# Loading packed weight codes and their scales as separate transfers in a fused attention and FFN block

## The chip, the cores and the metric

The kernel runs on one core of one Trainium2 chip. The metric is the device time of one execution in microseconds (us), taken as the median of the timed runs. The changed kernel is to be compared with the kernel before on the same chip.

## What is computed

The input `x` has 4 x 512 tokens of 512 channels, 2048 tokens in all. A first half adds a chunked, gated linear attention of `layernorm(x)` to `x`. A second half adds a gated FFN whose weights are stored as 4-bit codes, two in an int32 word, with one float scale for each block of 32:

```python
def dequant_nvfp4(W_packed, scales, block=32):
    low, high = W_packed & 15, W_packed >> 4 & 15
    idx = jnp.stack([low, high], axis=-1).reshape(N, -1)
    vals = NVFP4_LUT[idx].reshape(N, K // block, block) * scales[:, :, None]
    return vals.reshape(N, K)

Wg, Wu = dequant_nvfp4(gate_W_packed, ...), dequant_nvfp4(up_W_packed, ...)   # 4096 x 512 each
Wd = dequant_nvfp4(down_W_packed, ...)                                        # 512 x 4096
gate, up = xt @ Wg.T, xt @ Wu.T
gelu = jnp.tanh(0.7978845608 * (gate + 0.044715 * gate ** 3)) * gate * 0.5 + gate * 0.5
out = (gelu * up) @ Wd.T
```

## The kernel before

Every engine has a hand-written order of instructions, and semaphores tie the engines together. The attention part takes roughly the first quarter of the span. After that the FFN runs in eight groups of 512 hidden units (g = 0 to 7). Matrices are held as pairs of float16 parts (high and low), and three matmuls stand for one product. From tile 16 on the FFN is walked in pairs of hidden tiles (`m` = 8 to 63, eight pairs to a group). In each pair TensorE (PE) computes for `gate` and then for `up` seven block products P1 to P7, Strassen-like, with the down projection's products (`seven`, from m = 18 on, L695; `down`, L735, before and at the end) between them. ScalarE (ACT) copies partial results out of PSUM (`snapshot`, L1019), VectorE (DVE) adds to them (`combine`, L1376) and applies `inter` (L1269), ACT applies the gelu (L898), DVE adds down results into the rows of X1 (`into_rows`, L1304), and GpSimd (POOL) makes the low parts (L1601). `operand_sums` (L1314 to L1319) makes four differences of the finished pair on DVE, from pair 16 on in 46 pairs.

The weights come in 48 chunks of 128 x 512 codes, six to a group, numbered k. For a chunk the sync engine (SP) loads the codes into `raw` and the scales into `scl` (256 KB each; the scales are 8 rows, each repeated 16 times), from k = 10 on always into the same buffers. DVE's `dq_bits(k)` turns codes into float16 bits in a PSUM bank in four operations on 128 x 512 (L1330, L1332, L1335, L1338), one of which writes back into `raw`. `dq_finish(k)` multiplies them with the scales in two operations (L1359). ACT and POOL then split them into parts.

The order on DVE in a pair m, cut to what matters, is: `combine("gate", "C11")`, `dq_finish(k)` if a chunk is finished in this pair, `combine("gate", "C22")`, two `into_rows`, `dq_bits(k + 1)` if a chunk is finished in the next pair, `combine("gate", "C12")`. Chunks are finished in the pairs with m % 8 = 2, 3, 5, 6, 7 and 0, so that in the pairs with m % 8 = 2, 5, 6 and 7 a finish and the bits of the next chunk stand in one pair. After C12, ACT runs the gelu of the even tile and then the snapshot of P6 of `up`, for which PE's P7 of `up` waits.

SP's queue also moves rows of X1 to DRAM and back, 1 MB each (`kept`): in a pair with odd m it stores the rows of n = m // 2 - 1 after the last down product of n has been added (L1842), waits for the store to land, and fills the freed rows with those of n + 2 (L1846). The rows of n + 2 are needed from pair 2n + 6 on, that is m + 3.

Of the kernel before, what the change touches and what calls it, by code (L numbers as in the profile page):

```python
# [8 lines left out]
ALU = mybir.AluOpType  # L9
# [63 lines left out]
SEVEN = tuple(range(8, 31))  # L73
SEVEN_PAIRS = tuple(m for n in SEVEN for m in (2 * n, 2 * n + 1))
# [34 lines left out]
def row_done(n, tt):  # L109

    return 4 * n + tt + 1 - (4 * len(SEVEN) if n > SEVEN[-1] else 0)


def seventh(n, name):

    return 7 * (n - SEVEN[0]) + IN_TURN.index(name) + 1
# [19 lines left out]
def second(k):  # L136
    return not plain(k) and k % 2 == 1
# [18 lines left out]
def finished_in(k):  # L156

    return k - 2 if k < 12 else 8 * (k // 6) + (-6, -5, -3, -2, -1, 0)[k % 6]


FINISHED = {finished_in(k): k for k in range(10, 48)}
# [17 lines left out]
def block_kernel(nc, x, wqkv, bqk, bv, wab, bab, codes, scales, out, cla, kept):  # L179
    with ExitStack() as ctx:  # L180
# [3 lines left out]
        def sem(name):  # L184
            return ctx.enter_context(nc.semaphore(name))

        X1 = sb("X1", [128, NT, 512], F32)
# [8 lines left out]
        fw = sb("fw", [128, 2, 512], F32)  # L196
# [16 lines left out]
        def two(ap):  # L213
            return ap.rearrange("p (s n) -> p s n", s=2)
# [19 lines left out]
        tsum = E2[:, 0:1024].rearrange("p (t n) -> p t n", t=4)  # L234
# [8 lines left out]
        raw, scl = [load[:, j, :] for j in (0, 2)], [load[:, j, :].bitcast(F32) for j in (1, 3)]  # L243
# [75 lines left out]
        def row(n, tt):  # L319

            return 4 * (n % 4 if n < 4 else n % 2) + tt
# [13 lines left out]
        def floats(k):  # L335

            return wfs[pair_count(k) % 2 if k >= 12 else 0]

        def place(k):
            return k % 2 if k < 10 else 0  # L340

        def loaded(k):
            return 32 * (k // 2 + 1 if k < 10 else k - 4)

        def last_half(cut):
            return PS[0 if cut.start else bank_of["dn", NI // 4 - 1, 3]][:, 0:256]
# [7 lines left out]
        s_wv = [sem(f"s_wv{k}") for k in range(4)]  # L354
        s_k0 = sem("s_k0")
        s_const, s_out = sem("s_const"), sem("s_out")
        s_chunk = [sem(f"s_chunk{k}") for k in range(2)]
        s_setup = sem("s_setup")
        s_stat = {tag: sem(f"s_stat_{tag}") for tag in ("n1", "n2")}
        s_rstd = {tag: sem(f"s_rstd_{tag}") for tag in ("n1", "n2")}  # L360
# [16 lines left out]
        s_ihi, s_ilov, s_ilop, s_dn, s_ev = (sem(n) for n in ("s_ihi", "s_ilov", "s_ilop", "s_dn", "s_ev"))  # L377
        s_dq, s_whi, s_wlo, s_wl1 = (sem(n) for n in ("s_dq", "s_whi", "s_wlo", "s_wl1"))
# [3 lines left out]
        s_dsum, s_ohi, s_olo, s_seven, s_out7 = (sem(n) for n in ("s_dsum", "s_ohi", "s_olo", "s_seven", "s_out7"))  # L382
        s_half, s_done = sem("s_half"), sem("s_done")
        s_kept = [sem(f"s_kept{b}") for b in (2, 3)]
        s_store = [sem(f"s_store{i}") for i in range(2)]
# [447 lines left out]
        def _(eng):  # L833
# [58 lines left out]
            def gelu(i, pg, at=0):  # L892
                if i // 2 - 1 in SEVEN_PAIRS:
                    ac.wait_ge(s_olo, operand(i // 2 - 1, "o"))
                    ac.wait_ge(s_dsum, 4 * (i // 2 - 1 - SEVEN_PAIRS[0]) + 4)
                elif i >= 2:
                    ac.wait_ge(*ilo(i - 2))
                eng.activation(fw[:, i % 2, at:at + pg.shape[1]], pg, ACT.Gelu_apprx_tanh, scale=GS).then_inc(s_gelu, 1)  # L898
# [25 lines left out]

            def sums_high(m):
                for part in ("T01", "T23"):
                    ac.wait_ge(s_dsum, 4 * (m - SEVEN_PAIRS[0]) + 4)
                    eng.copy(part_of(m, 0, part), part_from(part)).then_inc(s_ohi, 1)  # L928

            def act_tile(i):  # L930
# [189 lines left out]
        def _(eng):  # L1120
# [184 lines left out]
                                         1.0 / (WS * IS), block_, ALU.mult, ALU.add).then_inc(s_out7, 1)  # L1305

            def operand_sums(m):
                e, o, at = fw[:, 0, :], fw[:, 1, :], 4 * (m - SEVEN_PAIRS[0])
                if m > SEVEN_PAIRS[0]:
                    dv.wait_ge(s_olo, operand(m - 1, "T23"))  # L1310
                else:
                    dv.wait_ge(s_kept[0], 16)
                dv.wait_ge(s_inter, whole(2 * m))
                eng.tensor_tensor(tsum[:, 0, :], e[:, 256:512], e[:, 0:256], ALU.subtract).then_inc(s_dsum, 1)  # L1314
                eng.tensor_tensor(tsum[:, 2, :], o[:, 256:512], e[:, 256:512], ALU.subtract).then_inc(s_dsum, 1)
                dv.wait_ge(s_dsum, at + 1)
                eng.tensor_tensor(tsum[:, 1, :], o[:, 256:512], tsum[:, 0, :], ALU.subtract).then_inc(s_dsum, 1)  # L1317
                dv.wait_ge(s_dsum, at + 3)
                eng.tensor_tensor(tsum[:, 3, :], o[:, 0:256], tsum[:, 1, :], ALU.subtract).then_inc(s_dsum, 1)  # L1319

            def dq_bits(k):

                s, codes_ = place(k), codes_in(k)
                dv.wait_ge(s_chunk[s], loaded(k))
                if k:
                    dv.wait_ge(s_dq, 6 * k)
                if k == 6:
                    for sm7, value in freed7:
                        dv.wait_ge(sm7, value)
                eng.tensor_scalar(codes_, raw[s], 4097, None, ALU.mult).then_inc(s_dq, 1)  # L1330
                dv.wait_ge(s_dq, 6 * k + 1)
                eng.tensor_scalar(raw[s], codes_, 12, -0x7FFF8000, ALU.logical_shift_left,  # L1332
                                  ALU.bitwise_and).then_inc(s_dq, 1)
                dv.wait_ge(s_dq, 6 * k + 2)
                eng.tensor_scalar(codes_, codes_, 9, 0x0E000E00, ALU.logical_shift_left,  # L1335
                                  ALU.bitwise_and).then_inc(s_dq, 1)
                dv.wait_ge(s_dq, 6 * k + 3)
                eng.tensor_tensor(codes_, codes_, raw[s], ALU.bitwise_or).then_inc(s_dq, 1)  # L1338

            def dq_finish(k):  # L1340
                s, dst = place(k), wf2 if second(k) else floats(k)
                dv.wait_ge(s_dq, 6 * k + 4)
                if second(k):
                    dv.wait_ge(s_wlo, WLO[k - 1][1])
                    if k == 7:
                        dv.wait_ge(s_turn["n2"], NT)
                    dv.wait_ge(s_wsum, pair_count(k) - 1)
                elif k in (12, 14):
                    dv.wait_ge(s_kept[1], 16)
                    dv.wait_ge(s_wlo, WLO[11][1])  # L1350
                    dv.wait_ge(s_wsum, 2)
                elif k > 14:
                    dv.wait_ge(s_wsum, pair_count(k) - 2)
                elif k and second(k - 1):
                    dv.wait_ge(s_wsum, pair_count(k - 1))
                for nib in range(2):
                    if 0 < k < 12 and not second(k) and not second(k - 1):
                        dv.wait_ge(s_wlo, WLO[k - 1][nib])
                    eng.scalar_tensor_tensor(dst[:, nib, :], codes_in(k).bitcast(F16)[:, nib::2], CODE, scl[s],  # L1359
                                             ALU.mult, ALU.mult).then_inc(s_dq, 1)  # L1360
# [405 lines left out]
        def _(eng):  # L1766
# [8 lines left out]
            def load_w(j):  # L1775
                eng.dma_start(wsrc[j], wv[:, :, 512 * j:512 * j + 512].rearrange("k p n -> p k n")).then_inc(s_w[j], 16)

            def load_chunk(k):
                s = place(k)
                if k >= 2:  # L1780
                    sp.wait_ge(s_dq, 6 * (k - 2 if k <= 10 else k - 1) + 6)
                eng.dma_start(raw[s], codes[k // 6, k % 6]).then_inc(s_chunk[s], 16)
                src = scales[k // 6, k % 6]
                rep = bass.AP(src.tensor, src.offset, [[512, 8], [0, 16], [1, 512]])
                eng.dma_start(scl[s], rep).then_inc(s_chunk[s], 16)

            def load_rows(T):
                if T >= 4:
# [35 lines left out]
                load_chunk(k)  # L1824
            sp.wait_ge(s_ev, 12)
            eng.dma_start(kept[2], X1[:, 8:12, :]).then_inc(s_kept[0], 16)
            for m in range(8, NI // 2):
                for k in range(10, 47):
                    if finished_in(k) == m:
                        load_chunk(k + 1)  # L1830
                n = m // 2 - 1
                if m == 9:
                    sp.wait_ge(s_ev, 16)
                    eng.dma_start(kept[3], X1[:, 12:16, :]).then_inc(s_kept[1], 16)
                elif m % 2 and n < 30:
                    if n in SEVEN:
                        sp.wait_ge(s_out7, seventh(n, "P4"))
                    else:
                        sp.wait_ge(s_ev, row_done(n, 3))
                    half_of = X1[:, row(n, 0):row(n, 0) + 4, :]  # L1840
                    home = ov[4 * (n % 4):4 * (n % 4) + 4].rearrange("t p d -> p t d") if n >= 28 else kept[n % 4]
                    eng.dma_start(home, half_of).then_inc(s_store[n % 2], 16)  # L1842
                    sp.wait_ge(s_store[n % 2], 16 * ((n - 4) // 2 + 1))
                    if n < 6:
                        sp.wait_ge(s_kept[n % 2], 16)
                    eng.dma_start(half_of, kept[(n + 2) % 4]).then_inc(s_fill[n % 2], 16)  # L1846
            for T in range(8, NT - 1):
                n = NI // 4 - 4 + T // 4
                if n in SEVEN:
# [48 lines left out]
```

## Time and profile before

| | |
|---|---|
| median of 2 timed runs | 1288.96 us (1288.34 to 1289.59) |
| the profiled execution, its own time | 1286.35 us |
| its span, first to last instruction | 1284.6 us |
| mean granted TensorE clock | 0.955 |
| PE busy | 1160.0 us (90%) |
| DVE busy | 847.9 us (66%) |
| ACT busy | 490.2 us (38%) |
| POOL busy | 647.3 us (50%) |
| DMA: queue of SP | 95.23 MB, 20.6% of 16 engines |

Busy times are those of one profiled execution and are averages over its stages. The span and the time of that execution differ by 1.75 us, which lies around the first and last instruction. A granted clock of 1 is 2.4 GHz, and 0.5 is 1.2 GHz.

### The profile page before, as it was taken

To read this page: it belongs to the slowest core of one execution; us is meant where nothing else is said; L and a number is where in the kernel's file an instruction comes from. 1 tells how busy PE (TensorE), PEld (TensorE's weight loads), DVE (VectorE), ACT (ScalarE), POOL (GpSimd) and SP (SyncE) were. 2 spreads that over 40 slices of the span, in tenths; PEclk is the share of its full clock that TensorE was granted. 3 is DMA by queue.
4 is the path that set the end of the run, shared out by engine and by line. 5 is a ranking of instruction groups with operands and counts; after the bars stand their busy time and mean duration, and the time that the engine had idled before them with its cause. 6 is when DMAs were issued, how large, how long until landed. Compare 5 with 4: busy or idle time off the path is not lost.

```text
span 1284.6 us, 22355 instructions
## 1 busy us (share of the span) xinstructions
PE 1160.0 (90%) x8842; PEld 884.5 (69%) x8842; DVE 847.9 (66%) x1537; ACT 490.2 (38%) x1148; POOL 647.3 (50%) x665
## 2 busy tenths in 40 slices
PE   9999999999989797987988798978897898879999
PEld 5566555654656565875877677867686786768887
DVE  8788574577665456665767676766676666766664
ACT  4423442532434243433433343424343343335342
POOL 3476342457656355544644563635455473547330
PEclk9999999999999899997999998999999898989999
DMA  7021010001022222220221222222222121221222
GB/s 271 10 67 58 12 47 18 9 17 66 18 82 81 85 99 82 83 99 28 105 92 66 90 83 83 99 83 100 82 83 99 62 111 59 83 66 66 96 94 76
DMA packets 30233, 96.66 MB, mean 75 GB/s; under 512 B 3440, under 2 KB 3760, under 8 KB 23472
## 3 DMA queue, kind: packets, MB, share of 16 engines
q1 hardware_dynamic: 30128, 95.23, 20.6%
q8 instruction: 70, 1.15, 0.3%
q14 instruction: 35, 0.29, 0.1%
HBM read 63.73 MB, written 31.49 MB: 74 GB/s over the span
## 4 chain that ended last, share of the span: by engine, by line
PE 59%; DVE 20%; DMA 10%; issue 6%; ACT 4%; SPq 1%; POOL 0%; DVEq 0%; POOLq 0%
PE ps L626 23%; PE ps L695 9%; DMA load<-scales 9%; PE ps L456 8%; PE ps L587 6%; PE ps L735 6%; DVE X L1317 2%; DVE fw L1269 2%; DVE load L1376 2%; DVE load L1332 2%; DVE ps L1335 2%; DVE ps L1330 2%; ACT fw L898 2%; DVE X L1304 1%; DVE bigB L1376 1%
## 5 line engine op out<-in xcount | busy, mean ns | idle before, releaser
L626 PE MATMUL ps<-REG,bigA 128*128 128x256 f16 x672 | 103.4, 296 | 115.3 <-ACT bigB L1019 115.2
L626 PE MATMUL ps<-REG,WR 128*128 128x256 f16 x1344 | 193.6, 283 | 0.0
L626 PE MATMUL ps<-XT,WR 128*128 128x256 f16 x1344 | 184.0, 273 | 0.0
L1019 ACT COPY load<-ps 128x256 f32<-128x256 f32 x168 | 62.5, 372 | 282.1 <-PE ps L626 282.0
L626 PEld LDWEIGHTS ps<-REG,bigA 128*128 128x128 f16 x672 | 66.3, 104 | 138.5 <-ACT bigB L1019 127.0
L1376 DVE TENSOR_TENSOR bigB<-bigB,ps 128x256 f32<-128x256 f32 x168 | 69.9, 416 | 133.4 <-ACT bigB L1019 102.3
L1601 POOL TENSOR_TENSOR ihl_s<-fw,ihl_s 128x512 f16<-128x512 f32 (+1 forms) x46 | 49.0, 1077 | 208.1 <-ACT ihl_s L922 208.1
L626 PEld LDWEIGHTS ps<-REG,WR 128*128 128x128 f16 x1344 | 135.7, 102 | 26.1 <-issue 1.3
L626 PEld LDWEIGHTS ps<-XT,WR 128*128 128x128 f16 x1344 | 132.1, 98 | 16.1
L898 ACT ACTIVATE fw<-load 128x256 f32<-128x256 f32 x112 | 58.7, 524 | 181.7 <-DVE load L1376 181.4
L1304 DVE SCALAR_TENSOR_TENSOR X<-ps,X 128x512 f32<-128x512 f32 x161 | 108.0, 682 | 18.1 <-PE ps L695 15.7
L1019 ACT COPY bigB<-ps 128x256 f32<-128x256 f32 x168 | 62.1, 370 | 89.0 <-PE ps L626 89.0
L695 PE MATMUL ps<-WR,ihl_s 128*128 128x256 f16 x684 | 91.8, 276 | 1.5 <-DVE X L1290 1.5
L1269 DVE SCALAR_TENSOR_TENSOR fw<-fw,ps 128x256 f32<-128x256 f32 (+1 forms) x72 | 34.4, 478 | 79.9 <-PE ps L626 47.9
L456 PE MATMUL ps<-XT,WR 128*128 128x512 f16 x384 | 86.8, 379 | 0.0
L1330 DVE TENSOR_SCALAR ps<-load 128x512 int32<-128x512 int32 x42 | 29.0, 691 | 86.0 <-DMA load<-scales 85.9
L1376 DVE TENSOR_TENSOR load<-load,ps 128x256 f32<-128x256 f32 x168 | 68.4, 410 | 25.8 <-ACT load L1019 19.0
L587 PE MATMUL ps<-XT,WR 128*128 128x512 f16 x384 | 85.0, 379 | 0.0
L1601 POOL TENSOR_TENSOR vv<-fw,vv 128x256 f16<-128x256 f32 (+1 forms) x46 | 42.4, 934 | 75.7 <-ACT vv L922 75.7
L1601 POOL TENSOR_TENSOR ihl_s<-X,ihl_s 128x512 f16<-128x512 f32 x46 | 52.9, 1161 | 48.5 <-ACT ihl_s L928 48.5
L695 PEld LDWEIGHTS ps<-WR,ihl_s 128*128 128x128 f16 x684 | 67.6, 99 | 10.3 <-DVE X L1290 1.8
L1269 DVE SCALAR_TENSOR_TENSOR fw<-fw,bigB 128x256 f32<-128x256 f32 x112 | 70.1, 626 | 3.9
(232 smaller groups left out, 2540.7 us busy)
## 6 DMA issues: line engine op xcount, KB each, us to landing
kept<-X SPq DMA_DIRECT2D x26, 1024.0 KB, 4.0
X<-kept SPq DMA_DIRECT2D x26, 1024.0 KB, 4.8
load<-codes SPq DMA_DIRECT2D x48, 256.0 KB
load<-scales SPq DMA_DIRECT2D x48, 256.0 KB
bigA<-cla SPq DMA_DIRECT2D x14, 256.0 KB, 3.1
X<-x SPq DMA_DIRECT2D x3, 1024.0 KB, 13.1
WR<-wqkv SPq DMA_DIRECT2D x2, 1024.0 KB, 9.7
y<-X SPq DMA_DIRECT2D x2, 1024.0 KB, 4.7
```

The costliest lines, as they stand in the source:

```text
L456: mm = eng.matmul(PS[bank][:, :], lhs, rhs, start=(n == 0), stop=(n == 11))
L587: mm = eng.matmul(bank[:, :], buf[:, wp, o + kt, 128 * j:128 * j + 128], XT[:, xp, kt, 512 * b:512 * b + 512], start=(n == 0), stop=(n == 11))
L626: mm = eng.matmul(half_bank(kind, name), w(wp, kt), x(xp, kt), start=(first and n == 0), stop=(n == 5), skip_group_check=True)
L695: mm = eng.matmul(PS[bank][:, 256 * tt:256 * tt + 256], x, weight(wp, u), start=(name in ("P1", "P2", "P5") and tt == u == ip == wp == 0), ...
L735: mm = eng.matmul(PS[bank][:, :], ih[:, ip, 128 * tt:128 * tt + 128], buf[:, wp, at(j), :], start=(j == 0 and p == 0), stop=(j == end and ...
L898: eng.activation(fw[:, i % 2, at:at + pg.shape[1]], pg, ACT.Gelu_apprx_tanh, scale=GS).then_inc(s_gelu, 1)
L1019: eng.copy(start, half_bank(kind, name)).then_inc(s_snap, 1)
L1269: eng.scalar_tensor_tensor(w, w, GS * IS, pu, ALU.mult, ALU.mult).then_inc(s_inter, 1)
L1304: eng.scalar_tensor_tensor(block_, PS[bank][:, :].rearrange("p (t u n) -> p t u n", t=2, u=2), 1.0 / (WS * IS), block_, ALU.mult, ALU.add) ...
L1330: eng.tensor_scalar(codes_, raw[s], 4097, None, ALU.mult).then_inc(s_dq, 1)
L1376: eng.tensor_tensor(c, c, half_bank(kind, end), ALU.add).then_inc(s_comb, 1)
L1601: eng.tensor_tensor(part_of(m, 1, part), part_from(part), part_of(m, 0, part), ALU.subtract).then_inc(s_olo, 1)
```

## The change

The codes and the scales of a chunk get a semaphore each, and are issued in separate steps. `dq_bits` waits for the codes alone and `dq_finish` for the scales alone. The codes of chunk k + 1 are issued as soon as `dq_bits(k)` is through (from k = 10 on), and no longer after `dq_finish(k)`. The scales of chunk k + 1 are still issued after `dq_finish(k)`. On SP the fill of rows moves from the odd pair, right behind its store, into the next pair, behind that pair's scales. Besides that, two of the four subtractions of `operand_sums` on 128 x 256 become one on 128 x 2 x 256, and its semaphore counts three steps and not four.

```diff
         def loaded(k):
-            return 32 * (k // 2 + 1 if k < 10 else k - 4)
+            return 16 * (k // 2 + 1 if k < 10 else k - 4)
...
             def operand_sums(m):
...
-                eng.tensor_tensor(tsum[:, 0, :], e[:, 256:512], e[:, 0:256], ALU.subtract).then_inc(s_dsum, 1)
-                eng.tensor_tensor(tsum[:, 2, :], o[:, 256:512], e[:, 256:512], ALU.subtract).then_inc(s_dsum, 1)
+                eng.tensor_tensor(tsum[:, 0::2, :], fw[:, :, 256:512], two(e), ALU.subtract).then_inc(s_dsum, 1)
                 dv.wait_ge(s_dsum, at + 1)
                 eng.tensor_tensor(tsum[:, 1, :], o[:, 256:512], tsum[:, 0, :], ALU.subtract).then_inc(s_dsum, 1)
-                dv.wait_ge(s_dsum, at + 3)
+                dv.wait_ge(s_dsum, at + 2)
                 eng.tensor_tensor(tsum[:, 3, :], o[:, 0:256], tsum[:, 1, :], ALU.subtract).then_inc(s_dsum, 1)
...
             def dq_bits(k):
-                dv.wait_ge(s_chunk[s], loaded(k))
+                dv.wait_ge(s_codes[s], loaded(k))
...
             def dq_finish(k):
                 s, dst = place(k), wf2 if second(k) else floats(k)
+                dv.wait_ge(s_scales[s], loaded(k))
...
-            def load_chunk(k):
+            def load_codes(k):
+                s = place(k)
+                if k >= 2:
+                    sp.wait_ge(s_dq, 6 * (k - 2) + 6 if k <= 10 else 6 * (k - 1) + 4)
+                eng.dma_start(raw[s], codes[k // 6, k % 6]).then_inc(s_codes[s], 16)
+
+            def load_scales(k):
                 s = place(k)
                 if k >= 2:
                     sp.wait_ge(s_dq, 6 * (k - 2 if k <= 10 else k - 1) + 6)
-                eng.dma_start(raw[s], codes[k // 6, k % 6]).then_inc(s_chunk[s], 16)
                 src = scales[k // 6, k % 6]
                 rep = bass.AP(src.tensor, src.offset, [[512, 8], [0, 16], [1, 512]])
-                eng.dma_start(scl[s], rep).then_inc(s_chunk[s], 16)
+                eng.dma_start(scl[s], rep).then_inc(s_scales[s], 16)
...
             for m in range(8, NI // 2):
-                for k in range(10, 47):
-                    if finished_in(k) == m:
-                        load_chunk(k + 1)
                 n = m // 2 - 1
+                if m < 10:
+                    load_codes(m + 3)
+                    load_scales(m + 3)
+                if m == 10:
+                    load_codes(13)
+                if m >= 10 and m in FINISHED and FINISHED[m] < 47:
+                    load_scales(FINISHED[m] + 1)
+                if m % 2 == 0 and 4 <= n - 1 < 30:
+                    fill_rows(n - 1)
+                if m >= 10 and m + 1 in FINISHED and FINISHED[m + 1] < 47:
+                    load_codes(FINISHED[m + 1] + 1)
...
                 elif m % 2 and n < 30:
-                    if n in SEVEN:
-                        sp.wait_ge(s_out7, seventh(n, "P4"))
-                    else:
-                        sp.wait_ge(s_ev, row_done(n, 3))
...
-                    sp.wait_ge(s_store[n % 2], 16 * ((n - 4) // 2 + 1))
...
-                    eng.dma_start(half_of, kept[(n + 2) % 4]).then_inc(s_fill[n % 2], 16)
+                    store_rows(n)
```

`store_rows` and `fill_rows` hold the same waits and transfers as the lines taken out.

SP's queue before, for pairs 21 to 23. `load<-codes` (L1782) and `load<-scales` (L1785) are a chunk's two transfers, first those of chunk 21. `kept<-X` is the store and `X<-kept` the fill; `s_dq` is the count that `dq_bits` and `dq_finish` raise.

```order
L1782 DMA load<-codes 128x512 [waits s_dq]
L1785 DMA load<-scales 128x1x512
L1842 DMA kept<-X 128x2048 [waits s_out7]
L1846 DMA X<-kept 128x2048 [waits s_store1]
L1782 DMA load<-codes 128x512 [waits s_dq]
L1785 DMA load<-scales 128x1x512
L1782 DMA load<-codes 128x512 [waits s_dq]
L1785 DMA load<-scales 128x1x512
L1842 DMA kept<-X 128x2048 [waits s_out7]
L1846 DMA X<-kept 128x2048 [waits s_store0]
```

The same pairs in the changed kernel; codes are now L1783, scales L1791, the store L1847, the fill L1853.

```order
L1791 DMA load<-scales 128x1x512 [waits s_dq]
L1783 DMA load<-codes 128x512 [waits s_dq]
L1847 DMA kept<-X 128x2048 [waits s_out7]
L1791 DMA load<-scales 128x1x512 [waits s_dq]
L1853 DMA X<-kept 128x2048 [waits s_store1]
L1783 DMA load<-codes 128x512 [waits s_dq]
L1791 DMA load<-scales 128x1x512 [waits s_dq]
L1783 DMA load<-codes 128x512 [waits s_dq]
L1847 DMA kept<-X 128x2048 [waits s_out7]
```

The scales of chunk 21 now stand ahead of the codes of chunk 22, which wait for `dq_bits(21)`; the codes of chunk 21 have been issued in pair 20. The fill has moved past the scales of pair 22.

DVE in pair 22 before, from `operand_sums` of pair 21 to `dq_bits(22)`: L1317 and L1319 are its last subtractions, L1376 the combines, L1359 `dq_finish(21)`, L1304 `into_rows`, and L1330 the first operation of `dq_bits(22)`.

```order
L1314 TENSOR_TENSOR X<-fw 128x256 [waits s_inter,s_olo]
L1315 TENSOR_TENSOR X<-fw 128x256
L1317 TENSOR_TENSOR X<-fw,X 128x256 [waits s_dsum]
L1319 TENSOR_TENSOR X<-fw,X 128x256 [waits s_dsum]
L1376 TENSOR_TENSOR load<-load,ps 128x256 [waits s_prod,s_snap]
L1359 SCALAR_TENSOR_TENSOR bigC<-ps,load 128x512 [waits s_wsum,s_wlo,s_dq]
L1359 SCALAR_TENSOR_TENSOR bigC<-ps,load 128x512
L1376 TENSOR_TENSOR load<-load,ps 128x256 [waits s_snap]
L1304 SCALAR_TENSOR_TENSOR X<-ps,X 128x4x128 [waits s_fill0,s_seven]
L1304 SCALAR_TENSOR_TENSOR X<-ps,X 128x4x128 [waits s_out7,s_seven]
L1330 TENSOR_SCALAR ps<-load 128x512 [waits s_dq,s_chunk0]
```

The same stretch in the changed kernel, where the lines from L1315 on are those of the new text.

```order
L1315 TENSOR_TENSOR X<-fw 128x2x256 [waits s_inter,s_olo]
L1317 TENSOR_TENSOR X<-fw,X 128x256 [waits s_dsum]
L1319 TENSOR_TENSOR X<-fw,X 128x256 [waits s_dsum]
L1377 TENSOR_TENSOR load<-load,ps 128x256 [waits s_prod,s_snap]
L1360 SCALAR_TENSOR_TENSOR bigC<-ps,load 128x512 [waits s_wlo,s_wsum,s_dq,s_scales0]
L1360 SCALAR_TENSOR_TENSOR bigC<-ps,load 128x512
L1377 TENSOR_TENSOR load<-load,ps 128x256 [waits s_snap]
L1305 SCALAR_TENSOR_TENSOR X<-ps,X 128x4x128 [waits s_fill0,s_seven]
L1305 SCALAR_TENSOR_TENSOR X<-ps,X 128x4x128 [waits s_out7,s_seven]
L1330 TENSOR_SCALAR ps<-load 128x512 [waits s_dq,s_codes0]
```

One instruction less stands there, `s_chunk0` at L1330 has become `s_codes0`, the first L1360 waits for `s_scales0` as well, and nothing else on DVE has changed places.

## Rows read from the trace of the kernel before

**Rows 1.** The cores' view: span and mean granted TensorE clock.

```profile
core 0: 1284.6 us, clock 0.955
```

**Rows 2.** The waits of the whole span: us in total, times, longest us.

```profile
PE ps L626 <- ACT bigB L1019: 115.2, 35, 7.2
...
DVE ps L1330 <- DMA load<-scales: 85.9, 24, 7.3
```

**Rows 3.** Timeline of pair 22: start us, us, engine; idle before and its releaser in brackets.

```profile
568.25 0.42 DVE L1314 TENSOR_TENSOR X<-fw 128x256 f32<-128x256 f32 x1
...
568.88 1.96 POOL L1601 TENSOR_TENSOR vv<-fw,vv 128x512 f16<-128x512 f32 x2 [10.63 <-ACT vv L922]
...
568.93 1.38 DVE L1317 TENSOR_TENSOR X<-fw,X 128x256 f32<-128x256 f32 x1
...
570.64 0.32 SPq L1846 DMA_DIRECT2D X<-kept  x1
...
571.37 1.27 DVE L1359 SCALAR_TENSOR_TENSOR bigC<-ps,load 128x512 f32<-128x512 f16 x2
...
572.67 0.33 SPq L1782 DMA_DIRECT2D load<-codes  x1
...
573.05 0.63 SPq L1785 DMA_DIRECT2D load<-scales  x1
...
577.74 0.69 DVE L1330 TENSOR_SCALAR ps<-load 128x512 int32<-128x512 int32 x1 [3.36 <-DMA load<-scales]
...
579.92 0.70 DVE L1338 TENSOR_TENSOR ps<-ps,load 128x512 int32<-128x512 int32 x1
...
580.98 0.63 ACT L898 ACTIVATE fw<-load 128x512 f32<-128x512 f32 x1 [5.68 <-DVE load L1376]
...
581.92 1.46 PE L626 MATMUL ps<-REG,bigA 128*128 128x256 f16 x6 [3.76 <-ACT bigB L1019]
```

**Rows 4.** Busy time by stretch: pairs 22, 25, 37, and pairs 58 and 59.

```profile
568.90:590.10 21.20, 17.44 (x136) 14.24 (x135) 12.91 (x24) 6.40 (x16) 10.24 (x10) 0.84 0.27 97
...
625.10:639.50 14.40, 13.63 (x126) 11.89 (x125) 11.39 (x22) 7.42 (x18) 9.97 (x10) 1.00 0.09 35
...
826.40:843.60 17.20, 13.32 (x123) 11.60 (x122) 12.26 (x24) 5.96 (x15) 6.64 (x7) 1.00 0.15 58
1191.50:1218.80 27.30, 27.30 (x252) 24.34 (x251) 17.77 (x34) 10.80 (x27) 8.43 (x9) 1.00 0.20 73
```

**Rows 5.** Busy time by stretch: the eight pairs 25 to 32, summed.

```profile
sum 137.00, PE 117.30 PEld 100.68 DVE 93.82 ACT 53.30 POOL 72.76; mean PE 29.33 PEld 25.17 DVE 23.45 ACT 13.32 POOL 18.19
```

**Rows 6.** PE busy in the 22 stretches at clock 0.5: first three, sum.

```profile
372.40:375.80 3.40, 3.13 (x11) 0.50 0.02 5
406.50:410.00 3.50, 3.50 (x14) 0.51 0.00 0
440.70:447.50 6.80, 3.99 (x13) 0.50 0.00 0
...
sum 116.20, PE 90.47; mean PE 4.11
```

**Rows 7.** Timeline of PE, 385 to 486 us: two of the stalls at P7.

```profile
405.54 0.83 PE L626 MATMUL ps<-REG,bigA 128*128 128x256 f16 x6 [2.47 <-ACT bigB L1019]
423.13 0.83 PE L626 MATMUL ps<-REG,bigA 128*128 128x256 f16 x6 [1.38 <-ACT bigB L1019]
```

**Rows 8.** Timeline of 340 to 386 us: bits of chunk 12, and PE behind them.

```profile
367.45 0.69 DVE L1330 TENSOR_SCALAR ps<-load 128x512 int32<-128x512 int32 x1 [2.44 <-DMA load<-scales]
...
372.67 1.46 PE L626 MATMUL ps<-REG,bigA 128*128 128x256 f16 x6 [4.79 <-ACT bigB L1019]
```

**Rows 9.** L1317 by source line: duration ns min/median/max.

```profile
L1317 DVE TENSOR_TENSOR X<-fw,X x46: 417/1382/1386, 481.4 to 1246.3; 128x256 f32<-128x256 f32 x46
```

**Rows 10.** Timeline of DVE, 980 to 984 us: the one short L1317, and L1319.

```profile
981.27 0.42 DVE L1317 TENSOR_TENSOR X<-fw,X 128x256 f32<-128x256 f32 x1
981.72 1.26 DVE L1319 TENSOR_TENSOR X<-fw,X 128x256 f32<-128x256 f32 x1
```

More of the change, by code:

```diff
@@ L356, in block_kernel @@
         s_const, s_out = sem("s_const"), sem("s_out")
-        s_chunk = [sem(f"s_chunk{k}") for k in range(2)]
+        s_codes = [sem(f"s_codes{k}") for k in range(2)]
+        s_scales = [sem(f"s_scales{k}") for k in range(2)]
         s_setup = sem("s_setup")
@@ L894, in gelu @@
                     ac.wait_ge(s_olo, operand(i // 2 - 1, "o"))
-                    ac.wait_ge(s_dsum, 4 * (i // 2 - 1 - SEVEN_PAIRS[0]) + 4)
+                    ac.wait_ge(s_dsum, 3 * (i // 2 - 1 - SEVEN_PAIRS[0]) + 3)
                 elif i >= 2:
@@ L926, in sums_high @@
                 for part in ("T01", "T23"):
-                    ac.wait_ge(s_dsum, 4 * (m - SEVEN_PAIRS[0]) + 4)
+                    ac.wait_ge(s_dsum, 3 * (m - SEVEN_PAIRS[0]) + 3)
                     eng.copy(part_of(m, 0, part), part_from(part)).then_inc(s_ohi, 1)
@@ L1307, in operand_sums @@
             def operand_sums(m):
-                e, o, at = fw[:, 0, :], fw[:, 1, :], 4 * (m - SEVEN_PAIRS[0])
+                e, o, at = fw[:, 0, :], fw[:, 1, :], 3 * (m - SEVEN_PAIRS[0])
                 if m > SEVEN_PAIRS[0]:
@@ L1781, in load_chunk @@
                     sp.wait_ge(s_dq, 6 * (k - 2 if k <= 10 else k - 1) + 6)
-                eng.dma_start(raw[s], codes[k // 6, k % 6]).then_inc(s_chunk[s], 16)
                 src = scales[k // 6, k % 6]
                 rep = bass.AP(src.tensor, src.offset, [[512, 8], [0, 16], [1, 512]])
-                eng.dma_start(scl[s], rep).then_inc(s_chunk[s], 16)
+                eng.dma_start(scl[s], rep).then_inc(s_scales[s], 16)
+            def load_chunk(k):
+                load_codes(k)
+                load_scales(k)
             def load_rows(T):
@@ L1826, in _, with home_of, store_rows, fill_rows @@
             eng.dma_start(kept[2], X1[:, 8:12, :]).then_inc(s_kept[0], 16)
+            def home_of(n):
+                if n >= 28:
+                    return ov[4 * (n % 4):4 * (n % 4) + 4].rearrange("t p d -> p t d")
+                return kept[n % 4]
+            def store_rows(n):
+                if n in SEVEN:
+                    sp.wait_ge(s_out7, seventh(n, "P4"))
+                else:
+                    sp.wait_ge(s_ev, row_done(n, 3))
+                eng.dma_start(home_of(n), X1[:, row(n, 0):row(n, 0) + 4, :]).then_inc(s_store[n % 2], 16)
+            def fill_rows(n):
+                sp.wait_ge(s_store[n % 2], 16 * ((n - 4) // 2 + 1))
+                if n < 6:
+                    sp.wait_ge(s_kept[n % 2], 16)
+                eng.dma_start(X1[:, row(n, 0):row(n, 0) + 4, :], kept[(n + 2) % 4]).then_inc(s_fill[n % 2], 16)
             for m in range(8, NI // 2):
-                for k in range(10, 47):
-                    if finished_in(k) == m:
-                        load_chunk(k + 1)
                 n = m // 2 - 1
+                if m < 10:
[9 more added lines that the diff above has]
+                    load_codes(FINISHED[m + 1] + 1)
                 if m == 9:
@@ L1835, in _ @@
                 elif m % 2 and n < 30:
-                    if n in SEVEN:
-                        sp.wait_ge(s_out7, seventh(n, "P4"))
-                    else:
-                        sp.wait_ge(s_ev, row_done(n, 3))
-                    half_of = X1[:, row(n, 0):row(n, 0) + 4, :]
-                    home = ov[4 * (n % 4):4 * (n % 4) + 4].rearrange("t p d -> p t d") if n >= 28 else kept[n % 4]
-                    eng.dma_start(home, half_of).then_inc(s_store[n % 2], 16)
-                    sp.wait_ge(s_store[n % 2], 16 * ((n - 4) // 2 + 1))
-                    if n < 6:
-                        sp.wait_ge(s_kept[n % 2], 16)
-                    eng.dma_start(half_of, kept[(n + 2) % 4]).then_inc(s_fill[n % 2], 16)
+                    store_rows(n)
             for T in range(8, NT - 1):
```

## The prediction

> **What bounds the kernel now.** I read the cores' view first: the span is 1284.6 us and the mean granted clock of TensorE is 0.955 [rows 1]. With only two levels, 1 and 0.5, that mean says that TensorE ran at 1.2 GHz for 2 x 0.045 x 1284.6 = 116 us. Both numbers of the story are there: PE is the engine with the most work, and it loses time to stalls and to a lowered clock.
>
> Then the waits [rows 2]. PE waits for one thing above all: 115.2 us in 35 stalls behind ACT's copy of P6 of `up`. DVE waits 85.9 us in 24 pieces at L1330, the first operation of `dq_bits`, for the DMA. The reader should ask whether these are the same time, and the timeline of pair 22 answers that [rows 3]. `dq_finish` starts at 571.37 and takes 1.27 us; only then, at 572.67 and 573.05, does SP issue the next chunk's codes and scales, which are through at 577.74, some 4.7 us after the second issue. DVE has stood still for 3.36 us by then. Four operations of bits follow, the last at 579.92, then C12, the gelu on ACT at 580.98, the snapshot, and PE resumes at 581.92 after a stall of 3.76 us. So the DMA wait stands inside PE's stall, and 3.76 - 3.36 = 0.40 us of the stall would be left without it.
>
> The stretches tell what a pair costs when nothing is late: pairs 58 and 59, in which nothing is dequantized, take 27.3 us together at full clock with PE always busy, 13.65 us each [rows 4]. Pair 22 takes 21.2 us at a mean clock of 0.84. Pair 25, which has bits and no finish just ahead of them, takes 14.4 us with 0.77 us of PE idle. This tells me that the bits alone cost little and the late transfer much.
>
> **The change, part by part.**
>
> *The codes' wait.* `dq_bits(k + 1)` stands in the same pair as `dq_finish(k)` in half of the pairs. Before, the load between them could not start until the finish was over. Now the codes are issued when `dq_bits(k)` is through, a pair earlier, some 14 us ahead at a pair's length of 14.4 us [rows 4], against less than 5 us that two transfers took [rows 3]. What SP moves past: the codes of the next chunk stand behind the scales (which wait for the finish, at the start of the pair) and, in even pairs, behind the fill, whose store was issued in the odd pair before; all of these come earlier in a pair than the bits, so the queue holds nothing up. The first of the waits is at 367.45, for chunk 12, 2.44 us inside a stall of 4.79 [rows 8]; there the codes are issued after the bits of chunk 11 and no longer after its finish, about 2 us sooner and without the scales behind them, so that I count it too. All 24 waits go: 85.9 us. In four of them PE's stall was shorter than DVE's wait, by up to 0.3 us (in the longest 7.2 against 7.3 [rows 2]), which takes off 0.9. **Term one: 85.0 us.** What is late next is DVE's own chain, 115.2 - 85.0 = 30 us of stall over 35 places, under 1 us each.
>
> *The clock.* The 22 stretches at 0.5 hold 116.2 us, in 90.47 of which PE was busy [rows 6]. Work done at half the clock takes twice as long, so half of the busy part is lost: 45.2 us. All but two of these stretches lie in or right behind a stall that held a DMA wait of those above. The two are the one at 406.50, behind a stall of 2.47 us that no DMA wait made [rows 6, 7], and the first one, at 372.40, where 4.79 - 2.44 = 2.35 us of stall stay [rows 8]; I leave both as they are, 3.13 and 3.50 us busy. That gives (90.47 - 6.63) / 2 = 41.9. I take the full value, since the stalls that stay are of the size of the one of 1.38 us at 423.13, after which no fall comes until 440.70, and since even 17.20 - 13.32 = 3.88 us of idle in pair 37 left the clock at 1.00 [rows 4, 6, 7]. **Term two: 41.9 us**, with 0 as its low end and 45.2 as its high end. As a check, pair 22 at clock 0.84 was slow for 0.16 x 2 x 21.2 = 6.8 us and so lost up to 3.4: 21.2 - 3.4 - 3.4 = 14.4 us or a little more, which is what pair 25 takes.
>
> *The fill.* It is issued in the next pair behind the scales, some 2 us later than the 570.64 of pair 22 [rows 3]. Its rows are needed three pairs, over 40 us, after the store's. Nothing: what hides it is these pairs, and were that cover gone the first `into_rows` would wait the 2 us.
>
> *The scales.* Issued as before, needed at the next finish, a pair or two on. Nothing is queued behind that wait that doesn't need it. 0.
>
> *The joined subtraction.* Before, L1314 starts at 568.25 and takes 0.42, and its twin runs until just past 568.93, where L1317 starts. An operation on 128 x 512 takes 0.70 (L1338) [rows 3], so the joined one ends at 568.95, and L1317 starts as before. L1317 then takes 1.38 us (median of 46 [rows 9]) because POOL's L1601 began at 568.88; that stays. I take 0, since the two starts differ by 0.02 us. The ends: in one pair L1317 came ahead of POOL, and it and L1319 took 0.42 + 1.26 = 1.68 us and not 2.15 [rows 10]. If the change brought that order, it would gain 0.47 us in each of the 30 pairs in which DVE's chain holds PE (20 with finish and bits, 10 with bits alone), 14 us. If the joined operation ran into POOL as L1317 does, it would cost 1.38 - 0.42 = 0.96 us there, 29 us.
>
> **The sum.** 85.0 + 41.9 = 126.9 us. Span: 1284.6 - 126.9 = 1157.7; that execution's own time 1286.35 - 126.9 = 1159.4. The median of the runs lies 2.6 us above that execution, so the forecast is **1162 us**. Is there room on the other engines? Eight pairs took 137.0 us with 93.8 us of DVE and 72.8 of POOL [rows 5]. The 126.9 us come out of some 800, so eight pairs shrink to about 115 us: DVE is then 82% busy and POOL 63%, and PE's floor is 8 x 13.65 = 109. Close, but nothing crosses.
>
> **The rivals.**
>
> *The clock doesn't recover.* Short stalls may go on lowering it: the one of 2.47 us did [rows 7]. The 30 us of stall that stay are spread over 35 places. Against it are the 1.38 us without a fall and pair 25 at 1.00 with its 0.77. If term two is nothing: 1162 + 42 = 1204; if half: 1183. The Trainium skill, "TensorE: Matmul & The Clock Gate", in its section on a second failure mode, tells of a kernel whose clock swung because PE idled briefly but often between groups of matmuls; by that rule this rival's 1204 would be the result. The rows at hand speak against it. Chance 0.10.
>
> *The joined subtraction collides with POOL*: 1162 + 29 = 1191. For it: 45 of 46 L1317 did collide. Against it: the joined one starts 0.6 us ahead of POOL [rows 3]. Chance 0.06.
>
> *The change doesn't do what it says*: codes are held back on SP, so that half of the waits and their falls stay, for instance in even pairs where the fill stands ahead of them. 1289 - 63 = 1226. The store had landed by 570.64, well ahead of the bits, which speaks against it. Chance 0.05.
>
> *Another engine takes over* (DVE's 82% leaves chains that don't fit) and the gain falls under 26 us: 1263 to 1289, chance 0.02.
>
> *Slower*: the finish now waits for scales alone, at the head of the pair, ahead of everything on DVE. With 37 finishes after the loads are split, a loss that eats the 127 us and more needs 3.4 us at each, that is scales that land over 14.4 + 3.4 = 18 us after their issue; the slowest thing seen is both transfers within 5 us [rows 3]. Beyond 18 us the kernel is slower than 1289. Chance 0.02.
>
> **How the numbers follow.** The forecast case, 0.75, is 1162 with ends from its own bounds: 14 us for the subtraction and 3.3 for the two kept falls below give 1145, and a third of term two above gives 1176. The range of 8 in 10 reaches on to the collision and to a half-recovered clock: 1145 to 1192; what lies above is half of the clock's case and the last three, 0.14. A measurement of this kernel can tell about 2% from no change, that is 1263 us: faster 0.95, the same 0.03, slower 0.02.
>
> **What would show it.** Right: no DMA wait at L1330, codes issued some 10 us ahead of their bits; PE's wait behind L1019 near 30 us; pairs with finish and bits at 14.3 to 15.2 us; mean clock about 0.99; L1317 still at 1.38 and L1315 at 0.70. Wrong in term two: waits gone and the clock at 0.96 or below. Wrong in the subtraction: L1315 at over 1 us. Wrong in the queue: SP issuing a chunk's codes less than 5 us ahead of its bits. The step that I trust least is that stalls of 1 to 2 us leave the clock alone.

## The result

The changed kernel takes 1159.74 us (median, 1159.74 to 1159.75) against 1288.96 us before. The ratio is 0.8998 with a 95% interval of 0.8959 to 0.9036: faster by 10%, 2.3 us from the forecast of 1162.

The cores' view of the changed kernel, beside [rows 1]:

```profile
core 0: 1157.6 us, clock 0.999
```

The waits of the whole span, beside [rows 2] (us in total, times, longest us). L1019 has become L1020 and L626 L627.

```profile
PE ps L627 <- ACT bigB L1020: 30.0, 31, 2.5
```

No line of DVE waiting for a DMA at L1330 is left. PE's stall behind ACT's copy has gone from 115.2 to 30.0 us, and the clock from 0.955 to 0.999. These are the two terms of the result, the stall and the clock; what follows shows how they hang together. The lines below are those of the profiled execution, 1159.75 us.

The timeline of pair 22, beside [rows 3]:

```profile
533.43 0.33 SPq L1783 DMA_DIRECT2D load<-codes  x1
...
539.06 0.69 DVE L1315 TENSOR_TENSOR X<-fw 128x512 f32<-128x512 f32 x1
...
539.78 1.34 DVE L1317 TENSOR_TENSOR X<-fw,X 128x256 f32<-128x256 f32 x1
...
542.19 1.27 DVE L1360 SCALAR_TENSOR_TENSOR bigC<-ps,load 128x512 f32<-128x512 f16 x2
...
543.49 0.63 SPq L1791 DMA_DIRECT2D load<-scales  x1
...
544.16 0.45 SPq L1853 DMA_DIRECT2D X<-kept  x1
...
545.11 0.68 DVE L1330 TENSOR_SCALAR ps<-load 128x512 int32<-128x512 int32 x1
...
547.28 0.70 DVE L1338 TENSOR_TENSOR ps<-ps,load 128x512 int32<-128x512 int32 x1
...
548.01 0.33 SPq L1783 DMA_DIRECT2D load<-codes  x1
...
548.33 0.63 ACT L899 ACTIVATE fw<-load 128x512 f32<-128x512 f32 x1 [2.52 <-DVE load L1377]
...
549.28 0.83 PE L627 MATMUL ps<-REG,bigA 128*128 128x256 f16 x6 [0.64 <-ACT bigB L1020]
```

The codes that `dq_bits` reads at 545.11 were issued at 533.43, 11.7 us ahead, in the pair before. The bits follow the rows' additions with no idle time, and PE's stall is 0.64 us and no longer 3.76. Six matmuls take 0.83 us and not 1.46: the clock is up.

Busy time by stretch: the only fall left, pairs 22 and 25, the eight pairs 25 to 32, pair 37, pairs 58 and 59, beside [rows 4 to 6]:

```profile
371.00:374.40 3.40, 3.40 (x13) 1.57 (x11) 0.84 (x2) 0.43 (x2) 0.73 (x1) 0.50 0.03 5
539.80:555.00 15.20, 14.56 (x134) 12.75 (x133) 13.30 (x22) 6.30 (x16) 10.22 (x10) 1.00 0.42 141
584.30:598.70 14.40, 13.63 (x126) 11.91 (x124) 11.34 (x20) 7.40 (x18) 9.97 (x10) 1.00 0.15 55
584.30:700.90 116.60, 111.30 (x1011) 97.45 (x1009) 93.90 (x161) 53.33 (x126) 72.81 (x66) 1.00 0.28 100
758.50:772.90 14.40, 13.30 (x123) 11.56 (x121) 12.09 (x22) 5.94 (x15) 6.61 (x7) 1.00 0.21 72
1064.50:1091.80 27.30, 27.30 (x253) 24.34 (x251) 17.70 (x31) 10.79 (x27) 8.42 (x9) 1.00 0.19 72
```

Pair 22 went from 21.2 to 15.2 us, pair 37, where no fall was to be recovered, from 17.2 to 14.4, and pair 25 and pairs 58 and 59, which had no DMA wait, took as long as before. Eight pairs take 116.6 us and not 137.0, with the same work on DVE (93.9) and POOL (72.8).

PE's row of the changed kernel's page splits the gain without any estimate, since PE has the same 8842 matmuls in both kernels:

```profile
PE 1117.3 (97%) x8842; PEld 862.1 (74%) x8842; DVE 848.7 (73%) x1491; ACT 489.4 (42%) x1148; POOL 646.9 (56%) x665
```

Its busy time fell from 1160.0 to 1117.3 us, which is 42.7 us for the same work, and the time in which it stood idle from 1284.6 - 1160.0 = 124.6 to 1157.6 - 1117.3 = 40.3 us, which is 84.3.

### The profile page after: what moved, and what is told of

It is laid out like the page before. It is cut to its first block, busy times and chain, and to the rows that moved or that the text cites. A ratio compares the mean times of both kernels' runs of the same rounds, so it can differ in the third digit from the quotient of the medians.

```text
span 1157.6 us, 22346 instructions
## 1 busy us (share of the span) xinstructions
PE 1117.3 (97%) x8842; PEld 862.1 (74%) x8842; DVE 848.7 (73%) x1491; ACT 489.4 (42%) x1148; POOL 646.9 (56%) x665
## 4 chain that ended last, share of the span: by engine, by line
PE 63%; DVE 24%; issue 7%; ACT 4%; DMA 1%; POOL 0%; DVEq 0%; SPq 0%; POOLq 0%
PE ps L627 24%; PE ps L696 9%; PE ps L457 9%; PE ps L588 7%; PE ps L736 7%; DVE X L1305 3%; DVE X L1317 3%; DVE fw L1270 3%; DVE load L1377 3%; DVE load L1332 2%; DVE ps L1335 2%; DVE ps L1330 2%; ACT fw L899 2%; DVE X L1315 2%; DVE bigB L1377 1%
## 5 line engine op out<-in xcount | busy, mean ns | idle before, releaser
L627 PE MATMUL ps<-REG,WR 128*128 128x256 f16 x1344 | 183.9, 273 | 0.0
L627 PE MATMUL ps<-XT,WR 128*128 128x256 f16 x1344 | 183.3, 273 | 0.0
L1020 ACT COPY load<-ps 128x256 f32<-128x256 f32 x168 | 62.5, 372 | 248.0 <-PE ps L627 247.9
L627 PEld LDWEIGHTS ps<-REG,WR 128*128 128x128 f16 x1344 | 130.4, 98 | 21.5 <-issue 0.6
L627 PEld LDWEIGHTS ps<-XT,WR 128*128 128x128 f16 x1344 | 131.5, 98 | 15.5
L627 PE MATMUL ps<-REG,bigA 128*128 128x256 f16 x672 | 92.0, 273 | 30.2 <-ACT bigB L1020 30.0
L627 PEld LDWEIGHTS ps<-REG,bigA 128*128 128x128 f16 x672 | 62.4, 98 | 49.1 <-ACT bigB L1020 40.6
L1020 ACT COPY bigB<-ps 128x256 f32<-128x256 f32 x168 | 62.1, 369 | 77.9 <-PE ps L627 77.9
L1270 DVE SCALAR_TENSOR_TENSOR fw<-fw,bigB 128x256 f32<-128x256 f32 x112 | 74.4, 665 | 3.9
L1270 DVE SCALAR_TENSOR_TENSOR fw<-fw,ps 128x256 f32<-128x256 f32 (+1 forms) x72 | 34.3, 477 | 50.4 <-PE ps L588 30.0
L588 PEld LDWEIGHTS ps<-XT,WR 128*128 128x128 f16 x384 | 37.6, 98 | 44.4
```

What stands on the lines that cost most here:

```text
L588: mm = eng.matmul(bank[:, :], buf[:, wp, o + kt, 128 * j:128 * j + 128], XT[:, xp, kt, 512 * b:512 * b + 512], start=(n == 0), stop=(n == 11))
L627: mm = eng.matmul(half_bank(kind, name), w(wp, kt), x(xp, kt), start=(first and n == 0), stop=(n == 5), skip_group_check=True)
L1020: eng.copy(start, half_bank(kind, name)).then_inc(s_snap, 1)
L1270: eng.scalar_tensor_tensor(w, w, GS * IS, pu, ALU.mult, ALU.mult).then_inc(s_inter, 1)
```

## The experiments

**The joined subtraction alone.** The kernel before with this and its counts:

```diff
-eng.tensor_tensor(tsum[:, 0, :], e[:, 256:512], e[:, 0:256], ALU.subtract).then_inc(s_dsum, 1)
-eng.tensor_tensor(tsum[:, 2, :], o[:, 256:512], e[:, 256:512], ALU.subtract).then_inc(s_dsum, 1)
+eng.tensor_tensor(tsum[:, 0::2, :], fw[:, :, 256:512], two(e), ALU.subtract).then_inc(s_dsum, 1)
...
```

> The kernel before with the joined subtraction alone. Theory (it costs nothing): 1289 us within 3, L1315 (the joined one) at 0.69 us and L1317 at about 1.34, ending when it did before. Rival (it runs into POOL's operation): 0.96 us more in 30 pairs, 1318 us. Rival (DVE gets ahead of POOL): 0.47 us less in 30 pairs, 1275 us.

1285.71 us (1280.57 to 1290.59), ratio to the kernel before 0.9982 (0.9961 to 1.0003): no change that can be told. By source line (duration ns min/median/max), the joined operation and then the next one:

```profile
L1314 DVE TENSOR_TENSOR X<-fw x46: 691/692/693, 478.5 to 1249.9; 128x512 f32<-128x512 f32 x46
```

```profile
L1316 DVE TENSOR_TENSOR X<-fw,X x46: 426/1336/1344, 479.2 to 1250.6; 128x256 f32<-128x256 f32 x46
```

The second still takes 1.34 us in the median; the shortest of 46 takes 0.43, against 0.42 before [rows 9]. In the changed kernel the two run from 539.06 to 539.78 + 1.34 = 541.12, 2.06 us; before, from 568.25 to 568.93 + 1.38 = 570.31, 2.06 us [rows 3]. Both rivals fall: one wanted 29 us more, the other 14 less.

**A semaphore each, nothing moved.** The kernel before, where `dq_bits` waits for the codes and `dq_finish` for the scales, but both are still issued after the last finish:

```diff
-eng.dma_start(raw[s], codes[k // 6, k % 6]).then_inc(s_chunk[s], 16)
+eng.dma_start(raw[s], codes[k // 6, k % 6]).then_inc(s_codes[s], 16)
...
-eng.dma_start(scl[s], rep).then_inc(s_chunk[s], 16)
+eng.dma_start(scl[s], rep).then_inc(s_scales[s], 16)
```

> The kernel before with a semaphore each for codes and scales and nothing moved: both are still issued after the finish of the last chunk. Theory (what costs is that the codes are issued late, and the scales behind them add a part): codes are through some 1.5 us before both are, so DVE waits 85.9 - 24 x 1.5 = 50 us, and about half of the clock's 42 us comes back: 1289 - 36 - 20 = 1233 us. Rival (codes and scales share the DMA engines and end together): 1285 us or more. Rival (the shared semaphore was all of it): 1162 us.

1233.90 us, ratio 0.9578 (0.9536 to 0.9620), as expected. Its waits:

```profile
PE ps L627 <- ACT bigB L1020: 81.3, 33, 5.8
...
DVE ps L1331 <- DMA load<-codes: 50.4, 22, 5.9
```

The wait falls from 85.9 to 50.4 us by the semaphore alone: the scales behind the codes had made up 35.5 us of it.

**Codes early, but the bits wait for both.** The changed kernel with

```diff
             def dq_bits(k):
                 dv.wait_ge(s_codes[s], loaded(k))
+                dv.wait_ge(s_scales[s], loaded(k))
```

> The changed kernel, but the bits wait for the scales of their chunk too. Theory (the scales are issued at the end of the finish and need some 3.5 us, the bits want them 1.6 us after their issue): DVE waits about 1.9 us at L1330 in some 20 pairs, 40 us, with few falls of the clock since the stalls stay near 3 us: 1160 + 40 to 1160 + 60, 1200 to 1220 us. Rival (the codes were all that was late, the order on SP does it): 1160 us.

1234.40 us, ratio 0.9575 (0.9544 to 0.9606), 14 us above the upper end of what was expected. Its waits:

```profile
PE ps L627 <- ACT bigB L1020: 78.9, 35, 4.1
...
DVE ps L1331 <- DMA load<-scales: 26.2, 14, 2.6
...
DVE ps L1331 <- issue: 21.9, 10, 2.4
```

The second line of DVE is the same wait, for which the profile names no releaser. Its timeline, pair 23:

```profile
574.17 0.63 SPq L1792 DMA_DIRECT2D load<-scales  x1
...
577.91 0.69 DVE L1331 TENSOR_SCALAR ps<-load 128x512 int32<-128x512 int32 x1 [2.24 <-issue]
```

So DVE waits 48 us and not 40, PE's stall is 48.9 us above the changed kernel's 30.0, and the clock is lowered in 14 stretches with 50.2 us of PE's work, which costs (50.2 - 3.4) / 2 = 23.4 us. I had reckoned with 40 for the stall and 0 to 20 for the clock. Each half of the change alone brings 54 us (this one has the moved fill and the joined subtraction too, which bring nothing by their own runs); together they bring 129, since half a wait still leaves stalls behind which the clock falls.

**PE kept busy in its stalls.** The kernel before, with matmuls whose results nobody reads:

```diff
+if kind == "up" and 10 <= m < 56 and m % 8 in (2, 5, 6, 7):
+    pe.wait_ge(s_gelu, piece(m, "C21"))
+    for _ in range(24):
+        eng.matmul(PS[2][:, 256:512], left(0, e0)(0, 0), toks(0, 0)(0, 0), start=True, stop=True, ...)
 pe.wait_ge(s_snap, pair_base(kind, m, 3) + 2)
 product("P7", comb(1), sums(2))
```

> The kernel before with 24 more matmuls of 128x256 (2.6 us) on PE ahead of the wait for P7 of up, in the pairs with a finish and bits; their results go to an unused half of a PSUM bank and are read by nobody. The DMA waits stay. Theory (the lowered clock is a cost of its own of 42 us, on top of the waits): PE has work while it stalls, the clock stays at 0.99, DVE still waits 84 us or so at L1330, and the time is 1289 - 42 = 1247 us. Rival (the falls cost nothing, since other work covers PE's slower matmuls): 1289 us. Rival (the fillers themselves delay P7): over 1289 us.

1258.21 us, ratio 0.9759 (0.9723 to 0.9794). Its waits:

```profile
DVE ps L1335 <- DMA load<-scales: 86.0, 24, 7.5
...
PE ps L626 <- ACT bigB L1024: 56.4, 33, 4.8
```

This is the run that tells the two terms apart. DVE waits for the DMA as long as before, 86.0 us, PE does 576 matmuls more, and the kernel is 30 us faster, with the clock at 0.988. It falls short of the 42 us since seven stretches at half the clock remain, behind what is left of the stalls, and this row sums them:

```profile
sum 30.80, PE 26.94; mean PE 3.85
```

(90.47 - 26.94) / 2 = 31.8 us. The stall that is left and the new matmuls take 56.4 + 576 x 0.109 = 119.2 us together, 4.0 more than the stall before, so that 27.8 us should be gained; the span is 25.8 us shorter and the median 30.1.

**The fill behind its store.** The changed kernel with the fill in its old place:

```diff
-                if m % 2 == 0 and 4 <= n - 1 < 30:
-                    fill_rows(n - 1)
...
                     store_rows(n)
+                    fill_rows(n)
```

> The changed kernel with the fill issued in the odd pair right behind its store, as before. Theory (the fill has three pairs to land and its place does nothing; SP only has to wait 4 us for the store at a time when the next scales are not yet wanted): 1160 us within 3, no DMA wait at L1330. Rival (waiting for the store on SP holds back the scales, or the fill runs into the codes, so that DVE waits again in the even pairs): 1170 us or more.

1159.88 us, ratio to the kernel before 0.9010 (0.8983 to 0.9038), the same as the changed kernel's. SP waits 96.0 us for the stores and not 39.5, and no wait of DVE for codes, scales or a fill appears in its list. The fill's new place does nothing that can be told.

**A longer chain on DVE.** The changed kernel, with two operations nobody reads:

```diff
                     dq_bits(FINISHED[m + 1])
+                    if m % 8 in (2, 5, 6, 7):
+                        dv.wait_ge(s_dq, 6 * FINISHED[m + 1] + 4)
+                        for j in range(2):
+                            eng.bn_stats(bst[:, j, :], PS[5][:, :])
```

> The changed kernel with two more operations on DVE (bn_stats of 128x512, 0.7 us each, read by nobody) behind the bits in the 24 pairs with a finish and bits. The stalls of PE at P7 grow from 0.6 to 1.6 us to some 2 to 3 us, often and regularly. Theory (short stalls leave the clock alone): 24 x 1.4 = 34 us more, 1194 us, with PE's wait at 64 us and the clock at 0.99. Rival (short and frequent stalls lower the clock as well, as with stalls of 4 us): a fall of 3.4 us or more behind each, 1235 us.

1202.55 us, ratio to the kernel before 0.9342 (0.9303 to 0.9381). PE's wait, and two of its stalls in the timeline:

```profile
PE ps L627 <- ACT bigB L1020: 60.9, 35, 3.6
```

```profile
1058.36 0.89 PE L627 MATMUL ps<-REG,bigA 128*128 128x256 f16 x6 [1.98 <-ACT bigB L1020]
1076.91 1.46 PE L627 MATMUL ps<-REG,bigA 128*128 128x256 f16 x6 [2.95 <-ACT bigB L1020]
```

The stretches of lowered clock behind them:

```profile
1059.00:1062.40 3.40, 3.40 (x18) 0.50 0.00 0
1076.10:1082.90 6.80, 5.99 (x29) 0.50 0.02 10
```

The truth lies between the two expectations: 31 us for the stalls, and 11 stretches at 0.5 in which PE was busy for 40.78 us, (40.78 - 3.40) / 2 = 19 us more than in the changed kernel. The first of them stands where the changed kernel has its only one, behind a stall of 3.59 us; the other ten stand behind stalls of 1.98 to 2.95 us. So stalls of 2 us among others of 2 to 3 can lower the clock, though of 19 such stalls only ten did. The profiled execution, 1207.39 us, was the slowest of the four.

**The bits behind C12.** From pair 10 on, in the changed kernel:

```diff
-                elif m + 1 in FINISHED:
-                    dq_bits(FINISHED[m + 1])
                 combine("gate", m, "C12")
                 combine("up", m, "C11")
+                if m >= 10 and m + 1 in FINISHED:
+                    dq_bits(FINISHED[m + 1])
```

> The changed kernel with the four operations of the bits moved on DVE from ahead of C12 of gate to behind C11 of up, from pair 10 on. Theory (what is left of PE's stall at P7 of up is the length of DVE's chain, of which the bits are 2.9 us): the 30 us of stall behind ACT's copy go to under 8, DVE's idle time behind that copy takes the bits up, and the time is 1138 us (1130 to 1145). Rival (the bits then delay what follows, C22 of up and the inter operations, and the stall turns up elsewhere): 1155 to 1175 us.

1136.23 us (1135.69 to 1137.09), ratio to the kernel before 0.8825 (0.8796 to 0.8854), below the changed kernel's interval. Its cores' view, and PE's waits at L627:

```profile
core 0: 1135.0 us, clock 1.000
```

```profile
PE ps L627 <- DVE bigB L1377: 6.0, 14, 0.4
...
PE ps L627 <- DVE load L1377: 5.2, 15, 1.2
...
PE ps L627 <- ACT bigB L1020: 0.9, 1, 0.9
```

Of 31 stalls behind ACT's copy one is left, at 352.64 us, ahead of pair 10 from which on the bits are moved. The rival's stall, 11.2 us behind DVE, is small. So DVE's chain with the bits in it was what still held PE, and this is the fastest version of the study.

**One sum for all of them.** If a kernel's span is the changed kernel's, plus its excess of stall over 30.0 us, plus half of its excess of PE's busy time at half the clock over 3.4 us, it should come out so:

| kernel | stall | busy at 0.5 | sum | span |
|---|---|---|---|---|
| before | 115.2 | 90.5 | 1286.3 | 1284.6 |
| joined subtraction | 113.9 | 101.5 | 1290.5 | 1288.9 |
| a semaphore each | 81.3 | 58.4 | 1236.4 | 1234.2 |
| PE kept busy | 56.4, and 576 matmuls of 0.109 | 26.9 | 1258.6 | 1258.8 |
| bits wait for both | 78.9 | 50.2 | 1229.9 | 1229.2 |
| fill at its store | 30.2 | 6.8 | 1159.5 | 1159.4 |
| longer chain | 60.9 | 40.8 | 1207.2 | 1205.7 |

All seven agree within 2.2 us. Stall and lowered clock add, and they leave no room for a third term of more than about 2 us. Six of the seven sums are 0.1 to 2.2 us too high, so both prices are slightly too dear: for the kernel before, PE's busy and idle times above give 42.7 and 84.3 us against the sum's 43.5 and 85.2. The kernel with the bits behind C12 is not in the table, since its stalls lie behind DVE; its PE is busy for 1114.7 us and idle for 20.3, that is 2.6 and 20.0 us less than in the changed kernel.

## Why the prediction was right

*The codes' wait*: forecast 85.0 us of stall gone and 30 left; measured 115.2 - 30.0 = 85.2 gone. All 24 waits went, the one of chunk 12 too, where 2.25 us of stall stayed against the 2.35 of the forecast. The 0.9 us taken off for stalls shorter than their DMA wait was misread: there are three such places and not four (418.94, 439.32 and 509.90 us), with 0.32 + 0.31 + 0.11 = 0.74 us. That it takes both the early issue and the separate semaphores, each good for 54 us alone, I had not worked out; the forecast needed only the two together.

*The clock*: forecast 41.9 us; measured (90.47 - 3.40) / 2 = 43.5. Of the two stretches that I kept, the first stayed (371.00) and the one behind the stall of 2.47 us did not come, though the stall did (2.48 us at 403.20). In the kernel with the fill at its store it came, so this one is probably a matter of the run. That the clock is a cost of its own is shown by the kernel with PE kept busy.

*The joined subtraction*: forecast 0, measured 0.00 us of difference in the pair of operations. *The fill and the scales*: forecast 0, shown for the fill's place by its own run; the scales cause no wait of DVE in the changed kernel.

*The weak step.* "Stalls of 1 to 2 us leave the clock alone" was named as the step trusted least, and it held with little to spare. The changed kernel's stalls between pairs 19 and 61 are at most 1.62 us and none brought a fall; with 1.4 us more on DVE those in the pairs with finish and bits became mostly 2.0 to 3.0, and ten stretches came back. The evidence that I gave for it, the 3.88 us of idle in pair 37 without a fall [rows 4], was worth less than I made of it, as one case among 24 stalls with a DMA wait, behind 21 of which the clock did fall. The same misjudgement is part of why the kernel whose bits wait for both came out above what I expected of it; the larger part, against the upper end, is the stall, 48.9 us and not 40. The rule of the Trainium skill on short and frequent idle stretches ("TensorE: Matmul & The Clock Gate", on a second failure mode) is borne out by the kernel with the longer chain (11 stretches at 0.5), though not by the changed kernel (one).

The longest of those stalls in the changed kernel, and the one in pair 37 of the kernel before:

```profile
797.93 0.83 PE L627 MATMUL ps<-REG,bigA 128*128 128x256 f16 x6 [1.62 <-ACT bigB L1020]
```

```profile
838.55 0.83 PE L626 MATMUL ps<-REG,bigA 128*128 128x256 f16 x6 [3.88 <-ACT bigB L1019]
```

*The two terms' sum* is 128.7 us; the span fell by 127.0 and the median by 129.2, for a forecast of 126.9. That the span was met to 0.1 us (1157.7 forecast, 1157.6 measured) is partly luck, since the clock's term was off by 1.6. What made the forecast of the median 2.3 us too high is the 2.6 us added because the median before lay that far above the profiled execution: that was the scatter of the kernel before, and in the changed kernel the two agree (1159.74 and 1159.75 against 1159.4 forecast for the profiled execution). The other rivals are refuted by the profile: no other engine took over (eight pairs in 116.6 us against the 115 of the forecast), and the codes weren't held back on SP (issued 11.7 us ahead of their bits in pair 22). No wait of DVE for scales is in its list.

## What to carry to other kernels

When an engine waits for a load, look at what the load itself waited for: here the buffer of the codes was free some 10 us before the load was issued (533.43 against 543.49 in the changed kernel's pairs 21 and 22), because the load was tied to the last reader of its sister buffer, and one semaphore tied its end to the slower of the two. A stall of PE can cost twice, once as idle time and once as about half of PE's busy time at the lowered clock behind it, and the two can be read from the profile and added. After the transfer was out of the way, the order on DVE was the next thing on the path: moving four operations of no urgency behind those that PE waits for brought another 23.5 us (1159.74 to 1136.23).

## What the runs showed of the hardware that was not expected

- The same stalls don't bring the same falls. The kernel before and the one with the joined subtraction have stalls of 115.2 and 113.9 us, but PE worked 90.5 and 101.5 us at 0.5, and the kernel before varies by 7.5 us over seven runs (1283.43 to 1290.92). The changed one agrees to 0.01 us, but over two runs only; with the fill at its store four runs lie at 1158.3 and 1161.5 us, with a mean clock of 1.000 and 0.997.
- The length of a stall alone doesn't tell whether the clock falls. It fell behind one of 1.98 us (1058.36 in the kernel with the longer chain) and stayed up behind one of 3.88 us (838.55 in the kernel before, in pair 37). Why is left open.
- Two DMAs of 256 KB, one right behind the other, are through by 4.7 us after the second's issue [rows 3]. The scales alone were waited for until 3.7 us after their issue (574.17 to 577.91, in the kernel whose bits wait for both).
